# A transformer block on one core: weight groups split once and kept, decoding in four steps, low parts on VectorE

## The reference

```python
mod = (silu(c) @ wmod).reshape(1, 6, 1, -1)              # six vectors of 256: sa, ca, ga, sb, cb, gb
ga, gb = sign(ga) * max(|ga|, 0.25), sign(gb) * max(|gb|, 0.25)
h = layernorm(x) * (1 + ca) + sa                         # x: 1024 rows of 256
x = x + ga * attention(h)                                # one head of 32, causal, rotary, compressed latent
h = layernorm(x) * (1 + cb) + sb
gate, up = h @ Wg.T, h @ Wu.T                            # 256 -> 2048
x = x + gb * ((gelu_tanh(gate) * up) @ Wd.T)             # 2048 -> 256
```

## Time and profile before

| | before |
|---|---|
| three runs | 236.59, 239.24 and 280.82 us; median 239.24 |
| profiled execution | span of 236.0 us from the first to the last instruction; its own time stands in no record, the lowest run is 236.59 |
| TensorE matmuls | 200.2 us busy, 85% of the span |
| VectorE | 162.0 us, 69% |
| GpSimd | 105.7 us, 45% |
| ScalarE | 84.9 us, 36% |
| transfers | mean share 0.01 of the transfer engines between 50 and 60 us, the weights are in; the output leaves in four pieces |

### The profile page before, as it was taken

How to read it: one execution, slowest core, us unless ns; L and a number is a source line. 1 busy time by engine, 2 the same in 40 slices (tenths; PEclk the granted TensorE clock), 3 DMA queues, 4 the chain that set the end, 5 groups by cost and what they waited for, 6 DMA issues and landing times. The chain is left out here.

```text
span 236.0 us, 3087 instructions
## 1 busy us (share of the span) xinstructions
PE 200.2 (85%) x1064; PEld 159.2 (67%) x1064; DVE 162.0 (69%) x265; ACT 84.9 (36%) x143; POOL 105.7 (45%) x78
## 2 busy tenths in 40 slices
PE   7797896997679575977786969997989999999992
PEld 2483584754458355766675858886769888888991
DVE  1676978779799999999999991259583333333334
ACT  2100405151757231415160507743614535525230
POOL 4430418060517563665775928646235256236200
PEclk9979975699999999999999799999999999999997
DMA  6999765200000000000000000000020000000002
GB/s 193 342 288 212 201 202 178 99 3 0 0 0 1 0 3 0 1 0 0 1 3 0 0 0 3 0 0 0 0 92 0 3 0 0 0 0 0 3 0 89
DMA packets 5645, 11.31 MB, mean 48 GB/s; under 512 B 544, under 2 KB 2752, under 8 KB 5632
## 3 DMA queue, kind: packets, MB, share of 16 engines
q1 hardware_dynamic: 5216, 10.82, 15.5%
q10 hardware_dynamic: 416, 0.33, 0.6%
HBM read 10.09 MB, written 1.05 MB: 47 GB/s over the span
## 5 line engine op out<-in xcount | busy, mean ns | idle before, releaser
L853 PE MATMUL ps<-H,WS 128*128 128x512 f32 x384 | 97.2, 397 | 18.9 <-DVE wmod_sb L707 16.7
L853 PEld LDWEIGHTS ps<-H,WS 128*128 128x128 f32 x384 | 69.6, 189 | 36.9 <-DVE wmod_sb L707 21.0
L853 PEld LDWEIGHTS ps<-WS,IS 128*128 128x128 f32 x384 | 50.9, 194 | 4.2 <-issue 2.1
L853 PE MATMUL ps<-WS,IS 128*128 128x256 f32 x384 | 52.2, 287 | 1.5 <-DVE wmod_sb L707 1.3
L404 ACT ACTIVATE IS<-wmod_sb 128x512 fp32r<-128x512 f32 x32 | 20.2, 632 | 85.3 <-DVE wmod_sb L707 52.0
L495 POOL TENSOR_TENSOR WS<-wbuf,WS 128x1024 fp32r<-128x1024 f32 x16 | 40.4, 2526 | 8.9 <-ACT WS L385 8.9
L500 POOL TENSOR_TENSOR WS<-wbuf,WS 128x512 fp32r<-128x512 f32 x16 | 22.9, 1433 | 39.8 <-ACT WS L392 39.8
L707 DVE TENSOR_TENSOR wmod_sb<-ps,wmod_sb 128x512 f32<-128x512 f32 x32 | 22.0, 687 | 26.6 <-PE ps L853 22.2
L277 POOL TENSOR_TENSOR IS<-wmod_sb,IS 128x512 fp32r<-128x512 f32 x14 | 20.7, 1479 | 27.8 <-ACT IS L404 25.6
L277 DVE TENSOR_TENSOR IS<-wmod_sb,IS 128x512 fp32r<-128x512 f32 x18 | 12.8, 710 | 24.9 <-ACT IS L404 24.2
L398 ACT ACTIVATE wmod_sb<-ps 128x512 f32<-128x512 f32 x32 | 18.8, 586 | 6.4 <-PE ps L853 6.4
(11 more groups left out here) (117 smaller groups left out, 215.3 us busy)
## 6 DMA issues: line engine op xcount, KB each, us to landing
wbuf<-packed SPq DMA_DIRECT2D x8, 384.0 KB
wbuf<-scales SPq DMA_DIRECT2D x8, 384.0 KB
xres<-x SPq DMA_DIRECT2D x2, 512.0 KB, 6.2
wmod_sb<-wmod SPq DMA_DIRECT2D x1, 1024.0 KB, 10.5
out<-xres SPq DMA_DIRECT2D x4, 256.0 KB, 2.2
wmod_sb<-wmod SPq DMA_DIRECT2D x1, 512.0 KB, 6.6
rope_sb<-rope SPq DMA_DIRECT2D x1, 512.0 KB, 11.1
cst<-consts SPq DMA_DIRECT2D x1, 322.0 KB, 4.9
```

Of the source, the lines that this page charges most:

```text
L853: return pe.matmul(o, lhsT, rhs, start=start, stop=stop)
```

## The change

WS is gone. WL (low parts of all eight groups) takes the place of the decoded weights in memory, and WH, WH6 and WH7 hold the high parts, so both are made once, in the first pass. To make room, several tiles lie on top of others: `under` allocates a tile whose memory the next one reuses (W under WL, PF under PL, rope_sb and chT under WH6, qk_h and prod under WH7), and xn holds one half in place of two. Decoding has four steps: each code is shifted to the top of the word and back by three with its sign kept, 768 elements each; one AND masks both halves, 1536 elements; one multiply applies the scale to 1536. `split_high(g)` on ScalarE is one copy of 1536. `weights_low(g)` is two subtractions of 768: on GpSimd for groups 0 and 1, on VectorE for 2 to 7, as part of what `decode_more` deals out: per group, two shifts in an even slot; low part of the group before, AND and multiply in the odd slot. `inter_low` is on VectorE for all units. TensorE's part is written out without its loop and waits for the weights in the first pass alone.

```diff
-DECODE_STEPS = 7
-EARLY = 2
-POOL_UNITS = 2 * (GROUPS - 1)
-STEPS_AT_START = 8
+DECODE_STEPS = 4
+EARLY = 3
+PERIOD = DECODE_STEPS + 1
...
+        def weights_low(engine, g, parts, done):
+            engine.wait_ge(w_hi, g + 1)
+            for e in parts:
+                engine.tensor_tensor(WL[:, g, e, :], W[:, g, e, :], high(g)[:, e, :].bitcast(F32),
+                                     ALU.subtract).then_inc(done, 1)
...
+            def split_high(g):
+                act.wait_ge(dec_done, g + 1)
+                if g >= GROUPS - 2:
+                    act.wait_ge(qk_ready, 4)
+                act.activation(high(g), W[:, g], ACT.Copy).then_inc(w_hi, 1)
...
-            split_gu(1, 1)
+            split_high(1)
             exps(1, 2 * HT - 1, 2 * HT)
-            split_d(1, 1)
+            split_high(2)

             for n in range(UNITS + 2):
-                G = n // 2 + 1
-                if n % 2 == 0 and G > 1:
-                    split_gu(G, G % GROUPS)
                 gelu(n, n % 2, n >= 2)
                 if n == 0:
                     out_high(1)
                 inter_hi(n, n % 2, n >= 2)
-                if n % 2 and G > 1:
-                    split_d(G, G % GROUPS)
+                g = EARLY + n // 2
+                if n % 2 and g < GROUPS:
+                    split_high(g)
...
-            low_gu(0, 0, 0)
-            low_d(0, 0, 0)
+
+            weights_low(pool, 0, range(2), w_lo_pool)
             rsqrt(N_LN2)
             for b in range(1, 2 * HT, 2):
                 probs_low(pool, 1, b, b + 1)
-            low_gu(1, 1, 1)
-            low_d(1, 1, 1)
-            for n in range(POOL_UNITS):
...
+            weights_low(pool, 1, range(2), w_lo_pool)
+            rsqrt(N_LN2 + 1)
...
                     if s == 0:
-                        dve.tensor_scalar(dec_a[:], bits, 0xFF, None, ALU.bitwise_and).then_inc(chain, 1)
+                        dve.tensor_scalar(dec[:, 0, :], bits, 28, 3, ALU.logical_shift_left,
+                                          ALU.arith_shift_right).then_inc(chain, 1)
                     elif s == 1:
-                        dve.tensor_scalar(dec_b[:], dec_a[:], 4097.0, None, ALU.mult).then_inc(chain, 1)
+                        dve.tensor_scalar(dec[:, 1, :], bits, 24, 3, ALU.logical_shift_left,
+                                          ALU.arith_shift_right).then_inc(chain, 1)
                     elif s == 2:
...
+                        dve.tensor_scalar(dec[:], dec[:], -0x72000000, None, ALU.bitwise_and).then_inc(chain, 1)
+
                     else:
...
+                        dve.scalar_tensor_tensor(W[:, g], vals, FP16_BIAS,
+                                                 W[:, g, 1, :].unsqueeze(1).to_broadcast([P, 2, WORDS]),
                                                  ALU.mult, ALU.mult).then_inc(dec_done, 1)
...
+                for q in range(first, last):
+                    g, step = EARLY + q // PERIOD, q % PERIOD
+                    if step == 2:
+                        weights_low(dve, g - 1, range(2), w_lo)
+                    elif g < GROUPS:
+                        step -= step > 2
+                        decode(g, step, step + 1)

             def steps_before(n):

-                return STEPS_AT_START + 2 * n if n <= 3 else STEPS_AT_START + 6 + 7 * (n - 3) // 2
+                return min(PERIOD * n // 2, PERIOD * (GROUPS - EARLY) + 3)
...
                 if n == 0:
                     out_stack(1)
-                elif n >= POOL_UNITS:
-                    if n == POOL_UNITS:
-                        dve.wait_ge(i_lo, n)
-                    inter_low(dve, n, n % 2)
-
+                inter_low(dve, n, n % 2, n >= 2)
...
+            def weights_ready(g):
+                pe.wait_ge(w_hi, g + 1)
+                if g < 2:
+                    pe.wait_ge(w_lo_pool, 2 * (g + 1))
+                else:
+                    pe.wait_ge(w_lo, 2 * (g - 1))
```

More of the change, by code:

```diff
@@ L72, in sb, with under @@
             return ctx.enter_context(nc.sbuf_tensor(name, shape, dt))
+        def under(name, shape, skip=0, dt=F32):
+            with nc.sbuf_tensor(name + "_skip", [P, max(skip, 4) // 4], F32) if skip else ExitStack():
+                with nc.sbuf_tensor(name, shape, dt) as t:
+                    return t
         def sem(name):
@@ L413, in _ @@
             v_high(1)
[L414 to L415 removed]
+            split_high(0)
             qk_high(1)
@@ L1039, in down @@
                             ins = mm(ps[:, Y + m, D * j:D * (j + 1)], IS[:, e, b, P * (2 * m + j):P * (2 * m + j + 1)],
-                                     WS[:, par, a, e, 2, :], first and q == j == 0, last and q == 2 and j == 1)
+                                     weights(a, g)[:, e, 2, :], first and q == j == 0, last and q == 2 and j == 1)
                     if last and m == 0:
@@ L1089, in _ @@
                 if b == 2 * HT - 2:
-                    gate_up(0, 0, 0, 0, 0, first=True, later=False)
+                    gate_up(0, first=True, later=False)
                 if b >= 2:
@@ L1095, in _ @@
             pe.wait_ge(gb_out, 1)
-            gate_up(1, 0, 0, 0, 1, later=False)
+            gate_up(1, later=False)
             attend(1, b - 1, k - 1)
             attend(1, b, k)
-            for n in range(2, UNITS + 3):
-                gate_up(n, n // 2, n // UNITS, n // 2 % 2, n % 2, first=n == UNITS, after_own_banks=n == 2)
+            for n in range(2, 2 * UNITS):
+                gate_up(n, first=n == UNITS, after_own_banks=n == 2)
                 if n == 2:
@@ L1106, in _ @@
                     transpose2(1)
-                d = n - 2
-                down(d, d // 2, d // UNITS, d // 2 % 2, d % 2, first=d % UNITS == 0, last=d == UNITS - 1)
-            with pe.Fori(0, 3) as it:
-                for j in range(4):
-                    u, d = 3 + j, 1 + j
-                    gate_up(4 * it + (UNITS + u), 2 * it + (GROUPS + u // 2), 1, u // 2 % 2, u % 2)
-                    down(4 * it + (UNITS + d), 2 * it + (GROUPS + d // 2), 1, d // 2 % 2, d % 2)
-            n = 2 * UNITS - 1
-            gate_up(n, n // 2, 1, n // 2 % 2, 1)
-            for d in (n - 2, n - 1, n):
-                down(d, d // 2, 1, d // 2 % 2, d % 2, last=d == n)
+                down(n - 2)
+            for d in (2 * UNITS - 2, 2 * UNITS - 1):
+                down(d)
 def kernel(**inputs):
```

138 lines of the change are left out of this document (44 added, 94 removed).

## The result

The changed kernel takes 254.81 us (median of 4 runs, 254.05 to 255.61), the kernel before 238.59 us in the same session (median of 4, 236.59 to 280.82). The ratio is 1.071, with a 95% interval from 1.065 to 1.077. Forecast were 248.3 us, a range of 240.5 to 256.0 and slower at 0.78: right in sign and inside the range, 6.5 us short in size. The profiled execution took 254.68 us with a span of 252.9 us, against a span of 236.0 us before, so the two traces differ by 16.9 us. Some executions of these kernels are longer, at a lower granted clock; medians are of all runs, while ratios and their intervals leave these executions out.

A forecast was written before the change was run, and what follows sets the result against it. VectorE's decoding, stretched by GpSimd, was taken to bound the first pass, TensorE the second. Terms -1.3 + 13.5 - 3.0 - 3.1 = +6.1 us, plus 3.0 for the clock, +9.1 on 239.24: 248.3 us, range 240.5 to 256.0.

The forecast's parts named there:

- What bounds the kernel: First pass bound by VectorE's decoding and GpSimd's low parts together, 10.9 us a pair; second pass at TensorE's own pace.
- The wait that the change adds: After each group VectorE stands still for ScalarE's split_high plus gelu, 2.2 us; pair 12.25 us, 1.35 more than before.
- Decoding steps: On VectorE, undisturbed: shifts of 768 take 0.56 us, the AND over 1536 0.96, the multiply over 1536 1.76.
- rival (c): VectorE's new shifts and AND run slower, 1.6 us per group, five groups, +8: 256 us; chance 0.09.
- Rival (b): ScalarE's split doesn't end the wait, VectorE decodes well before gelu; the five stalls vanish: 234.3 us, faster; chance 0.08.
- The pair: First pass, VectorE: even unit 3.3 us, odd unit 6.75, together 10.05; with the 2.2 us wait 12.25.
- TensorE's clock: Idle 3.9 us per pair lets the clock fall behind gaps; half of five at 1.2 us taken, +3.0.
- rival (a): TensorE at half clock behind every one of five gaps: +6.1 + 8.5, 253.8 us; chance 0.20.
- Units 10 to 12: No decoding left, TensorE is next: 7.5 us against 10.55 before, -3.0.
- Units 12 to 18: 27.1 us against 30.2 before, -3.1, from shorter residual2 and gate_floor and no weight splits ahead of the gelus.
- From unit 19 on nothing changes: Second pass stays at TensorE's own pace, one unit every 4.18 us, its matmuls unchanged: difference 0.
- The start: inter_full(0) starts at 79.5 us against 80.77, -1.3; GpSimd's low parts of group 1 not later than gelu(0) by anything that counts.

The follow-up runs named there:

- e1: Changed kernel with split_high of groups 3 to 7 moved from behind inter_hi of the odd unit to behind inter_hi of the next even unit; 233.40 us.
- e7: Changed kernel with only the order of inter_low and VectorE's decoding pieces turned round, split_high left ahead of the next gelu; 241.70 us.
- e2: Changed kernel with idle matmuls of a zeroed tile on TensorE ahead of gate of units 5, 7, 9 and 11; 247.63 us.
- e5: As e1, with the high part of group 2 also moved from ahead of the first gelu to behind inter_hi of unit 0; 238.31 us.

## Why the prediction was right, and where its sizes were off

- **What bounds the kernel**: right. From unit 19 on the units are 4.2 us apart after as before (to 0.04 us), so keeping the split groups through the second pass, which is what they are kept for, has no time to save there.
- **The wait that the change adds**: right, in its place (ahead of every even unit), its chain (multiply, high part, gelu) and its size: 2.09 us of idle VectorE against 2.2. e1 shows that it is the cause: take it away and 21 us go. e7 adds that it costs as much only within the longer loop: shorten the rest of the loop by 2.2 us a pair and 15 us go with the stall left in place.
- **Decoding steps**: right to 0.01 us (0.55, 0.95, 1.76 against 0.56, 0.96, 1.76); rival (c), with 8 us for slow steps, is refuted. Rival (b), a split that is not last, is refuted by the 0.03 us between multiply and high part; e1 is what it would have looked like, and it priced it at 234.3 us.
- **The pair**: 12.25 us forecast, 12.45 with the clock kept up (e2). Inter_low of the odd unit waits 1.51 us for inter_hi, where I took the second pass's 0.75, so it comes 0.7 us later than counted; 0.5 of that was counted too much elsewhere and cancels, which is luck.
- **TensorE's clock**: here the size was off. I took half of five falls at 1.2 us, +3.0, from the kernel before, where one gap in five was followed by one. All five gaps were. Filling four of them is worth 7.2 us (e2), so a fall costs about 1.8 us. The rule of the Trainium skill that I had weighed and put second (TensorE: Matmul & The Clock Gate, "HAM oscillation — how this bites in real kernels") describes what happened here behind the five gaps of 3.75 to 6.11 us, and rival (a) is the mechanism that came on top of the forecast. Its 8.5 us were the nearer figure. The 254.81 us lie 1.0 above rival (a)'s 253.8 and inside the range by the room that the high end of 256 gave to rival (c), which didn't come: in part that is luck. The row of the kernel before (gaps of 2.2 us) was not near enough to a gap of 3.75 us to price it.
- **Units 10 to 12**: -3.0 forecast, -0.3 measured. It is the same term: the fifth gap, at 152.57 us, lies at the head of this stretch, and with it filled the stretch takes 7.6 us (e2: 147.73 to 155.34), the 7.5 of the prediction.
- **Units 12 to 18**: -3.05 against -3.1, right.
- **"From unit 19 on nothing changes"**: wrong by 1.4 us: 1.0 at the border, where TensorE's own order (scale_out, down(16), gate(19)) now bounds up(19), and 0.5 over units 19 to 31, of which the cause stays open.
- **The start**: -0.8 against -1.3; the attention stage was itself 1.1 us later in the profiled execution, behind a fall of the clock at 22 to 28 us. e5 shows that ScalarE's high part binds inter_full(0) (3.4 us sooner without it), but GpSimd's low parts bind gate(2), and that is what reaches the end.
- **The time around the span** is 1.8 us (254.68 less 252.9), where I had taken 0.6 from the lowest of three runs. It cancels in the differences.

The spans differ by 7.8 us more than the +9.1 of the prediction: 5.8 of it in units 0 to 12, 1.4 from unit 18 on and 0.5 at the start. Of the 5.8 e2 shows at least 4.2 to be the clock (7.2 less the 3.0 forecast). Most of the remaining 1.6 is in units 2 to 4: 15.55 us forecast, 16.98 with the four gaps filled. Their own gap, of 6.1 us, was not filled, so how they divide between clock and order of work is open.
